# Cross attention's scores as 32 by 32 tiles at sixteen places of the array, without zero-padded queries

## The reference, cut to what matters

```python
def _L0_xattn_ref(queries, keys, values):      # (32, 32, 512), (32, 257, 512) twice
    q = _split_heads(queries)                  # 16 heads of 32
    k = _split_heads(keys)
    v = _split_heads(values)
    scores = jnp.einsum('bhqd,bhkd->bhqk', q, k) * scale
    weights = jax.nn.softmax(scores, axis=-1)
    out = jnp.einsum('bhqk,bhkd->bhqd', weights, v)
    return out.transpose(0, 2, 1, 3).reshape(B, S, H * Dh)

x = x + _L0_xattn_ref(_layernorm(x, axis=-1), ctx_1024, ctx_1024)
x = x + _L0_attn_ref(_layernorm(x, axis=-1), ...)
x = x + _L0_ffn_ref(_layernorm(x, axis=-1), ...)
```

## Time and profile before

| | us |
|---|---|
| median of 3 runs (lowest, highest) | 2545.91 (2543.9, 2551.46) |
| the profiled execution, its own time | 2545.14 |
| its span | 2543.3 |
| busy: PE, PEld | 2448.7, 1963.1 |
| busy: DVE, ACT, POOL | 1978.2, 1678.3, 635.1 |

### The profile page before, as it was taken

One profiled execution on the slowest core, in us unless ns is written; L12 is line 12 of the kernel. 1 busy time (PEld: TensorE's weight loads), 2 busy tenths in 40 slices (PEclk: granted clock), 3 DMA queues, 4 the chain that ended last, 5 costly groups with the idle time before them and its releaser, 6 DMA issues.

```text
span 2543.3 us, 53248 instructions
## 1 busy us (share of the span) xinstructions
PE 2448.7 (96%) x21914; PEld 1963.1 (77%) x21914; DVE 1978.2 (78%) x1878; ACT 1678.3 (66%) x2107; POOL 635.1 (25%) x541
## 2 busy tenths in 40 slices
PE   6877989998999999999999999999999999999998
PEld 5763458776888888888888888888888888888886
DVE  6764458665799889998978988988778877867795
ACT  5551233334688878887867887877667777766784
POOL 3410010001132333332222233223222222222221
PEclk9998999998999999999999999999999999999999
DMA  6770023234899999998978999999888888878894
GB/s 201 212 232 0 2 77 139 86 151 175 297 374 386 359 345 385 377 378 327 379 285 325 369 354 349 387 353 344 305 295 326 325 305 321 326 296 282 313 370 133
DMA packets 128524, 714.96 MB, mean 281 GB/s; under 512 B 15488, under 2 KB 23808, under 8 KB 52416
## 3 DMA queue, kind: packets, MB, share of 16 engines
q1 hardware_dynamic: 102048, 665.96, 67.9%
q0 software_dynamic: 26144, 44.06, 8.4%
HBM read 684.46 MB, written 25.49 MB: 279 GB/s over the span
## 4 chain that ended last, share of the span: by engine, by line
PE 75%; issue 0%; DVE 0%; POOL 0%; ACT 0%; ACTq 0%; POOLq 0%; DVEq 0%
PE ps L1465 14%; PE ps L1467 14%; PE ps L1466 14%; PE ps L1543 7%; PE ps L1545 7%; PE ps L1544 7%; PE ps L1496 5%; PE ps L1515 4%; PE ps L1528 3%; PE ps L1453 1%; PE ps L1506 1%; PE ps L1456 0%; DVE e_WL L1356 0%; ACT e_WH L1274 0%; POOL out_rows L1427 0%
## 5 line engine op out<-in xcount | busy, mean ns | idle before, releaser
L1356 DVE TENSOR_TENSOR e_WL<-ring,e_WH 128x2048 fp32r<-128x2048 f32 x462 | 1057.2, 2289 | 233.7 <-ACT e_WH L1274 228.7
L1274 ACT ACTIVATE e_WH<-ring 128x2048 fp32r<-128x2048 f32 x462 | 885.0, 1916 | 125.3 <-PE ps L1467 56.9
L1465 PE MATMUL ps<-e_WH,e_XEh 128*128 128x512 f32 x1536 | 605.1, 394 | 3.6 <-DVE e_XEl L1378 3.6
L1467 PE MATMUL ps<-e_WH,e_XEl 128*128 128x512 f32 x1536 | 599.2, 390 | 0.0
L1466 PE MATMUL ps<-e_WL,e_XEh 128*128 128x512 f32 x1536 | 598.7, 390 | 0.0
L1415 POOL TENSOR_TENSOR e_tick<-e_tick 128x1 f32<-128x1 f32 x126 | 111.6, 886 | 1304.5 <-ACT X L1322 1253.8
L1465 PEld LDWEIGHTS ps<-e_WH,e_XEh 128*128 128x128 f32 x1536 | 289.0, 188 | 62.1 <-DVE e_XEl L1378 4.0
L1467 PEld LDWEIGHTS ps<-e_WH,e_XEl 128*128 128x128 f32 x1536 | 288.8, 188 | 61.2
L1466 PEld LDWEIGHTS ps<-e_WL,e_XEh 128*128 128x128 f32 x1536 | 289.1, 188 | 58.0
L1543 PE MATMUL ps<-e_WH,e_GTh 128*128 128x512 f32 x768 | 318.9, 415 | 0.8 <-issue 0.8
L1356 DVE TENSOR_TENSOR e_WL<-e_more,e_WH 128x2048 fp32r<-128x2048 f32 x114 | 260.8, 2289 | 53.9 <-ACT e_WH L1274 52.4
(11 more groups left out here) (207 smaller groups left out, 3198.8 us busy)
## 6 DMA issues: line engine op xcount, KB each, us to landing
ring<-in_experts SPq DMA_DIRECT2D x462, 1024.0 KB, 8.3
e_more<-in_experts SPq DMA_DIRECT2D x114, 1024.0 KB, 8.4
ring<-in_shared SPq DMA_DIRECT2D x12, 1536.0 KB, 6.2
a_K<-in_ctx_k SPq DMA_DIRECT2D x32, 514.0 KB, 5.2
a_V<-in_ctx_v SPq DMA_DIRECT2D x32, 384.0 KB
a_V<-in_ctx_v SPq DMA_DIRECT2D x32, 130.0 KB
X<-in_x SPq DMA_DIRECT2D x4, 512.0 KB, 4.9
xn_scratch<-ring SPq DMA_DIRECT2D x1, 2048.0 KB, 7.9
```

The lines of the kernel that those rows point to most:

```text
L1274: act.activation(WH[:, nth % HELD, :], unit(i), ACT.Copy).then_inc(hi_done, 1)
L1356: dve.tensor_tensor(WL[:, at, :], unit(place(kind, n)), WH[:, at, :], ALU.subtract).then_inc(lo_done, 1)
L1465: pe.matmul(dst, h, wh, start=(k == 0), stop=False)
L1467: last = pe.matmul(dst, l, wh, start=False, stop=(k == G - 1))
```

## The change

The scores of a head are now a matmul of their own: 32 rows (the head's features), the head's queries out of XT as weights (32 columns), its rows of K moving (257 columns). Its output lies in bank g as before, but in the partitions of column group (g + h) mod 4 in place of h. So the 16 heads of a batch lie at 16 different places of the array: row group h, column group (g + h) mod 4. The buffer Q, its zeroing, GpSimd's copies and the semaphores q_ready and zeroed are gone. Maxima, exponentials, scaling and transposes take all partitions and stay; the value matmuls read their head's columns of PTa and PTb at the new place.

```diff
-            Q = sb("a_Q", [P, 4, G, P])
...
-                pool.memset(Q[:, :, :, :], 0.0).then_inc(zeroed, 1)
...
-                pool.wait_ge(zeroed, 1)
-
-                for b in range(B):
-                    i = b % 4
-                    if i == 0:
-                        pool.wait_ge(xt_copied, b // 4 + 1)
-                    if b >= 4:
-                        pool.wait_ge(s_done, 2 * (b - 3))
-                    for h in range(4):
-                        r = slice(32 * h, 32 * h + 32)
-                        pool.tensor_copy(Q[r, i, :, r], XT[r, :, SQ * b:SQ * (b + 1)]).then_inc(q_ready, 1)
...
+                def column(g, h):
+
+                    c = (g + h) % 4
+                    return slice(32 * c, 32 * c + 32)
+
                 def scores(b):
+
                     i = b % 4
-                    pe.wait_ge(q_ready, 4 * b + 4)
                     pe.wait_ge(k_in[i], 16 * (b // 4) + 16)
+                    at = slice(SQ * b, SQ * (b + 1))
                     for g in range(G):
                         if b >= 1:
                             pe.wait_ge(exp_done, 4 * (b - 1) + g + 1)
-                        last = pe.matmul(ps[:, g, 0:SK], Q[:, i, g, :], K[:, i, g, :], start=True, stop=True)
+                        for h in range(4):
+                            r = slice(32 * h, 32 * h + 32)
+                            last = pe.matmul(ps[column(g, h), g, 0:SK], XT[r, g, at], K[r, i, g, :], start=True, stop=True,
+                                             skip_group_check=True)
                         if g % 2 == 1:
                             last.then_inc(s_done, 1)
...
-                                pt = PTa[0:KC, b % 2, k, g, r] if k < 2 else PTb[:, b % 2, g, r]
+                                q = column(g, h)
+                                pt = PTa[0:KC, b % 2, k, g, q] if k < 2 else PTb[:, b % 2, g, q]
```

More of the change, by code:

```diff
@@ L177, in program @@
             made = sem("a_made")
-            zeroed = sem("a_zeroed")
             ident_ready = sem("a_ident_ready")
-            q_ready = sem("a_q_ready")
             s_done = sem("a_s_done")
```

## The result

The change made the kernel slower by a quarter of a per cent: 2550.82 us in the median of 18 runs (2547.1 to 2559.3), against 2544.71 (2540.14 to 2551.89) for the kernel before on the same chips; the ratio is 1.0023, with an interval of 1.0014 to 1.0031. The forecast, 2538.5, had the sign wrong, and the time lies just above its range. The profiled execution of after has a span of 2551.4 us, 8.0 more than before.

A forecast was written before the change was run, and what follows sets the result against it. The prediction took the cross-attention loop to be bound by a cycle of waits. Its terms, 7.2 + 1.0 (GpSimd's copies gone) + 0.7 - 1.5 - 0.5 = 6.9 us, took 2545.14 to 2538.2; forecast 2538.5, range 2534.5 to 2550.

The forecast's parts named there:

- Instructions: TensorE's instruction stream in the cross-attention loop: more matmuls and loads to fetch a batch, put at 0.5 us of loss.
- fetching becomes the bound: Rival: instruction fetches of 4.5 us a piece set the loop's turn at 5.0 us, 2550 in all; chance 0.07.
- Scores: Cross-attention score matmuls: tiles finish the first half sooner, VectorE's 0.18 us wait goes and 0.07 us overlaps, 7.2 us gained.
- K: K's loads in the loop: a shorter turn makes more of them late, a loss of 1.5 us, bounds 0 and 4.
- Start: Scores of batches 0 and 1, openly waited for at the loop's start, come sooner: 0.7 us gained.
- The clock falls: Rival: TensorE, less busy in the loop, drops to half clock, about 20 us over half the turns, 2558; chance 0.08.
- End of stage: End of cross attention: the stream grows by six whole pieces, so the three halts stay where they are; no change.
- Four tiles at a time: Rival: only four score tiles work at once, so scores take as long as before; 2548, no change; chance 0.15.
- banks: Rival: row tiles exclude each other in a bank, so scores take 6.9 us a turn, 2686 in all; chance 0.03.

The follow-up runs named there:

- experiment 5: The kernel before, with K sent one turn sooner, ahead of V in SyncE's list; ratio 0.9988 to the kernel before, 2542.42 us.
- experiment 8: The kernel before with K sent one turn sooner and only head groups 0 and 1 in 32x32 tiles, 260 instructions a batch; ratio 0.9979, 2541.58 us.
- experiment 3: The changed kernel without 12 value matmuls a batch, plus one unused whole-array matmul, 240 instructions; only cross attention compared, 29 turns in 137.4 us.
- experiment 7: The changed kernel with GpSimd's query copies kept, though nothing reads them; 2554.38 us.
- experiment 2: The thinned kernel: the changed kernel without 12 value matmuls a batch, 236 instructions, output incomplete; only cross attention compared, 29 turns in 139.6 us.
- experiment 4: The changed kernel with K sent one turn sooner, ahead of V in SyncE's list; ratio 1.001 to the kernel before, 2548.28 us.
- experiment 9: The changed kernel with K sent one turn sooner, columns g ^ h, value matmuls for two heads at once, 188 instructions; ratio 0.9979, 2539.14 us.
- experiment 10: The kernel of experiment 9 with two of its four small output copies moved from VectorE to ScalarE; ratio 0.9945 to the kernel before, 2532.46 us.
- experiment 6: The changed kernel without the column rotation, so all four head groups use the same four tiles; 2558.95 us.
- experiment 1: The kernel before with 12 small unused matmuls a batch added, 284 instructions in place of 236; ratio 1.009, 2568.57 us.

## Why the prediction was wrong

**The step that failed is *Instructions*.** I had its parts: 16 KB pieces, some 250 instructions in each, 4.5 us for a fetch, 284 instructions in a 4.5 us turn. But I compared means, 4.1 us a piece against a fetch of 4.5, and let TensorE's spare 0.5 to 0.9 us take up the difference: 0.5 us. The sum should have gone by place. A piece that holds TensorE's wait ahead of the transposes lasts 4 to 5 us; the one that doesn't is gone in 2.2, and then the stop is 3 us, three times its spare. Such pieces couldn't exist with 236 instructions a batch. The rows for it were there: the halts of rows 9 are just such places, value matmuls in a rush. Halts, with the half clock and the late K that came behind them, are 14.1 us in the loop where I had 0.5. A part is still missing: why some packets start late, and why some kernels whose pieces all hold the wait halt all the same, for 0.6 to 2.0 us (experiments 5 and 8 with K ahead, once also experiment 3). The rival *fetching becomes the bound*, 2550, names the right resource and happens to hit the time, but by the wrong sum: clean turns were 4.51, not 5.0.

*Scores, K and start.*
- Scores: all sixteen tiles work (1.05 us in all), L331 follows the PTb copy at once, the turn is 4.51 where 4.47 was forecast: right within 0.04 a turn. The split was off: of the 0.24 us some 0.11 is GpSimd's (experiment 7, one execution), the tiles' own about 0.13, and not 0.25.
- K: 1.5 us more was forecast. In after two turns show it alone (5 and 13, 1.6 us over clean), since halts delay the need for K as well; without halts it is 6.1 us (experiment 3), 3 more than before, within the bounds.
- Start: forecast 0.7 us sooner; the third scores come 1.05 us later (first weight load 29.60, before 28.55). The clock is 0.50 from 23.5 to 30.4 us and again from 33.8 on for 3.4 us, where rows 10 have 1.00 with TensorE 3.50 of 5 us busy. In after it is 2.63 of the same 5 us; but the tiled kernels of experiments 2, 3, 4, 7, 9 and 10 have 2.62 to 2.64 there too and keep 1.00. With them the time from the first scores to the third is 7.2 to 7.3 us, with the whole-array scores of before 7.5, in after 8.9: so the shorter scores are worth 0.3 us at the start, not 0.7, and this fall of the clock costs 1.7, in the profiled execution at least. The stretch in after:

```profile
20.00:40.00 20.00, 12.77 (x261) 8.13 (x260) 12.01 (x25) 11.63 (x36) 0.00 (x0) 0.74 0.38 93
```

- *The clock falls* had 0.08. By itself it costs some 7 us in the thinned kernel, and it is a good part of the loss here: 20.5 us at half clock again. By the thinned kernel's rate that would be, as an estimate, some 7 of the 19 us lost between turns and at the start. 10.2 us of the 20.5 come with no halt ahead of them (from 23.5 and from 33.8 on); how the rest shares its turns with the halts stays open.
- *End of stage*: the three halts stand at the very same instructions (88th, 125th, 187th of the last three batches), as forecast, and this part is 18.3 us against 18.8.
- *Four tiles at a time* and *banks*: refuted by after itself; experiment 6 is what four tiles give. In a clean turn the 32 recorded score matmuls start within 0.67 us, 22 ns apart in the mean, where whole-array ones are 217 ns apart: ten times. One after another, the eight of a bank would take 8 x 0.217 = 1.7 us, and all 32 are over in 1.05. The Trainium skill, TensorE: Matmul & The Clock Gate, "Measured speedup vs the span model", has 10.6 for sixteen tiles, and the trace agrees. The Trainium skill, TensorEngine Tiling (Array Packing), "Gotcha 1: PSUM Pressure", says that different row tiles cannot access the same bank at once. That does not hold here, where four row tiles at four different column places write each bank.

The deviation adds up, with the first weight loads of before (28.55 to 169.67) as a base: 29 turns 13.4 us over the forecast 134.9 (12.2 lost between turns, 1.2 for 0.04 a turn), the start 1.75, the end -0.5, the stages behind +0.4: 15.0, and the profiled executions differ by 8.0 where -6.9 was forecast.

## What to carry to other kernels

Count the instructions that an engine runs between two of its long waits, not only those a turn: while a loop has fewer than a fetched piece holds (256 here), every piece holds a wait that covers all of the fetch or most of it (no halt in the kernel before, five of 0.6 to 1.2 us with K ahead); with more, some piece can run through without one, and it stops the engine for most of a fetch (3 of 5.3 us). So cutting a matmul into smaller ones has a price in instructions, and what is cut in one place can be paid by merging in another, as with the paired values. And TensorE, made less busy, may lose its clock (experiments 2 and 3): look what it did just before each fall.

## What the runs showed that was not expected

- Fetching: 64 bytes an instruction, 256 a packet; a stop falls on the 256 grid, to the instruction, and lasts up to 4.0 us (experiment 1, at 195.3). The changed kernel has 278 packets on queue 8, the one with paired values, with 96 instructions a batch less, 266. In the stop that ends at 64.84, K and V are not what TensorE waits for: from 62.3 on the DMA engines move nothing but the packet.
- Sixteen 32x32 tiles with 257 columns of float32 take 1.05 us; four at a time 1.94; 16 matmuls of 32 rows into four banks with four columns do not exclude each other.
- TensorE, 104 of 146 us busy, was at half clock for 20.5 us with no halt ahead of it (experiment 2); with 116 to 141 (experiments 3, 6, 8, 9 and 10) for 3.4 us at most, near 32 us or behind a halt; with 125 (experiment 1) for 10.2 us, all behind halts.
- With few instructions and K ahead the loop runs like clockwork: 29 turns are within 0.3 and 0.7 us of 29 median ones (experiments 9 and 10).
